# A second product of the one-hot tile with itself, ahead of the degree product, on TensorE during setup

## The reference, cut to what matters

```python
deg_out = segment_sum(w, s); deg_in = segment_sum(w, d)        # with self loops
wn = w * rsqrt(deg_out)[s] * rsqrt(deg_in)[d]
for _ in range(10):
    h = 0.9 * segment_sum(h[s] * wn[:, None], d) + 0.1 * feat_0
x = layernorm(x + h)
score = exp(clip(sum(K[src] * Q[dst] / sqrt(8) * E, -1), -5, 5))   # 8 heads of 8
x = layernorm(x + segment_sum(V[src] * score, dst))
```

## Time and profile before

| what | us |
|---|---|
| median of three runs | 9977.31 |
| the profiled execution's own time | 9976.81 |
| its span | 9975.0 |
| first degree product starts (line 2330) | 161.5 |
| last degree product starts (line 2330) | 1568.1 |
| flag is written (line 2092) | 1641.1 |

### The profile page before, as it was taken

The page is one execution under the profiler, slowest core; times in us unless marked ns, Lnnn a source line. Parts: engine busy times, 40 slices in busy tenths (PEclk is TensorE's granted clock), DMA queues, the critical chain, the costliest instruction groups (busy, mean ns, idle before and its releaser), DMA issues.

```text
span 9975.0 us, 144406 instructions
## 1 busy us (share of the span) xinstructions
PE 8829.3 (89%) x50368; PEld 4786.6 (48%) x50368; DVE 4943.6 (50%) x14438; ACT 5539.0 (56%) x7215; POOL 7255.4 (73%) x7701
## 2 busy tenths in 40 slices
PE   3999997999999999999999999999999766666666
PEld 2777774333333333333333333333333465655665
DVE  7666663443444434444344443444434455566666
ACT  1333334787777777777777777777777411111111
POOL 5677776777777777777777777777777377777776
PEclk5555556999999999999999999999999777777676
DMA  9972225999999999899999999999999565555554
GB/s 359 394 279 64 74 71 174 347 344 310 347 310 347 339 317 347 309 346 334 323 347 309 347 326 331 348 308 348 318 336 342 167 162 143 143 145 143 143 143 119
DMA packets 1378005, 2669.54 MB, mean 268 GB/s; under 512 B 683776, under 2 KB 713379, under 8 KB 1377270
## 3 DMA queue, kind: packets, MB, share of 16 engines
q1 hardware_dynamic: 958006, 2245.72, 63.3%
q0 software_dynamic: 248000, 261.74, 10.7%
q10 hardware_dynamic: 171264, 152.74, 5.3%
HBM read 2426.96 MB, written 232.42 MB: 267 GB/s over the span
## 4 chain that ended last, share of the span: by engine, by line
PE 42%; POOL 39%; issue 14%; DMA 3%; DVE 2%; ACT 1%; SPq 0%; POOLq 0%; DVEq 0%; ACTq 0%
PE banks L2369 25%; POOL arena L1646 23%; POOL arena L1660 15%; PE banks L2330 10%; PE banks L2420 3%; PE banks L2332 3%; DMA arena<-node_rows,src_idx 1%; PE banks L2413 1%; DMA x_sb<-in_edge_weight_dram 1%; PE banks L2447 1%; DMA u_sb<-key_rows 1%; DMA arena<-dense 0%; POOL dense L1622 0%; DVE arena L1934 0%; POOL arena L1642 0%
## 5 line engine op out<-in xcount | busy, mean ns | idle before, releaser
L1646 POOL DMA_INDIRECT arena<-node_rows,src_idx x4800 | 4582.3, 955 | 1583.8 <-issue 1452.0
L1716 ACT ACTIVATE arena<-arena 128x1024 f32<-128x1024 f32 x4900 | 4762.2, 1044 | 1380.2 <-DMA arena<-dense 1224.3
L2369 PE MATMUL banks<-arena 128*64 128x512 f32 x12240 | 2715.0, 595 | 19.8 <-ACT arena L1716 19.5
L2369 PE MATMUL banks<-arena,u_sb 128*64 128x512 f32 x11760 | 2613.1, 596 | 82.3 <-ACT arena L1716 82.0
L1660 POOL DMA_INDIRECT arena<-kv_rows,src_idx x1568 | 1503.1, 959 | 597.2 <-issue 477.7
L2103 DVE TENSOR_SCALAR arena<-banks,rel,w_tab 128x128 f32<-128x128 f32 x4800 | 1603.5, 403 | 123.2 <-DVE arena L2120 99.6
L2369 PEld LDWEIGHTS banks<-arena 128*64 128x64 f32 x12240 | 877.0, 138 | 1544.4 <-issue 1467.8
L2369 PEld LDWEIGHTS banks<-arena,u_sb 128*64 128x64 f32 x11760 | 844.4, 138 | 1552.3 <-issue 1467.6
L2330 PE MATMUL banks<-arena 128*128 128x98 f32 x3136 | 1174.7, 478 | 93.0 <-ACT arena L1695 92.9
L1622 POOL DMA_INDIRECT dense<-arena x1012 | 980.4, 969 | 370.8 <-issue 314.6
L1765 ACT ACTIVATE banks<-arena 128x64 f32<-128x64 f32 x196 | 44.6, 228 | 1694.6 <-DVEq L2248 1694.6
(11 more groups left out here) (241 smaller groups left out, 6399.4 us busy)
## 6 DMA issues: line engine op xcount, KB each, us to landing
arena<-dense SPq DMA_DIRECT2D x3550, 512.0 KB
dense<-blank SPq DMA_DIRECT2D x5, 26112.0 KB, 189.5
arena<-in_dst_dram SPq DMA_DIRECT2D x195, 512.0 KB
arena<-node_rows,src_idx POOLq DMA_INDIRECT x4800
arena<-in_edge_attr_dram SPq DMA_DIRECT2D x195, 256.0 KB, 3.2
u_sb<-key_rows ACTq DMA_DIRECT2D x26, 1792.0 KB
dense<-blank SPq DMA_DIRECT2D x1, 44800.0 KB, 195.0
arena<-key_rows ACTq DMA_DIRECT2D x23, 1792.0 KB
```

The source lines that it names most:

```text
L1646: gp.indirect_dma_start(out=rows_in[:, n % ROWS, s, :], out_offset=None, in_=node_rows[k % 2], in_offset=bass.IndirectOffsetOnAxis(ap=src_ ...
L1716: nc.scalar.activation(planes[:, q % PLANES, half, :], ring[:, n % SLOTS, :], ACT.Relu, scale=-1.0 if half else 1.0).then_inc(planes_act, 1)
L2369: done = mm(banks[h * D:(h + 1) * D, sum_slot(k, g), :], u, rows[:, h * 512:(h + 1) * 512], start=first, stop=last, tile_position=(0, h * ...
```

## The change

One product is added per tile in `setup_pe`, ahead of the wide degree product: `hot_lo` of the tile as weights (128 columns) and as the moving operand (128 columns), written to columns 0 to 127 of PSUM bank 0 with `start` and `stop` set. Nothing reads that result. No wait and no semaphore update is added or moved.

```diff
@@ -2325,6 +2325,7 @@
             pe.wait_ge(hots_scaled, n + 1)
             for t in range(HB):
                 col = n * HB + t
+                mm(banks[:, 0, 0:P], hot_lo[:, n % 2, t, :], hot_lo[:, n % 2, t, :], start=True, stop=True, skip_group_check=True)
                 s0 = BASE[col // 2] // QUART
                 end = n == HOT_BATCHES - 1
                 mm(banks[:, 4, 0:NB], hot_lo[:, n % 2, t, :], hot_hw[:, n % 2, t, 0:NB], start=False, stop=end and t == HB - 1, skip_group_check=True)
```

## The result

The changed kernel takes 10621.48 us (median of 4 runs, 10619.44 to 10627.08) against 9977.3 us, a ratio of 1.0645 with a 95% interval of 1.0631 to 1.0659. It is 644 us slower; the forecast was 648 us more, 10625 us. The profiled execution has a span of 10617.7 us, 642.7 more than before.

What follows compares the result with a forecast made beforehand. The prediction took TensorE to bound the setup loop at 1.2 GHz: 669 us for the added pairs less 21 us of filled idle time, 648 us more, gave 10625 us. The range was 10565 to 10685 us.

Steps and rivals of the forecast that it cites:

- TensorE is the bound of the setup and nothing hides the added work: Setup's degree-product loop: TensorE busy 250.00 of 250 us, so added products lengthen the setup, by 648 us net.
- the 32 that were given as the most: End of setup: GpSimd's scatters set the limit, so a faster TensorE could bring back at most 32 us.
- The price of the pair, two record paces of 0.213 us: Each tile of the degree-product loop grows by 0.427 us, from 0.88 to 1.31; 669 us over 1568 products.
- The second rival: Degree-product loop: the added pair costs more, 0.68 to 0.86 us, giving 11017 to 11300 us; chance 3%.
- The idle time that fills: Degree-product loop: the added work fills 21 of the 26.5 us that TensorE idles, which is taken off the cost.
- The clock stays at 1.2 GHz: Degree-product loop: TensorE's granted clock stays at 0.50 all through, despite the added products.
- The first rival: Degree-product loop: the added stream raises TensorE to 2.4 GHz, GpSimd sets the end, 9945 us; chance 6%.
- The third rival: Degree-product loop: shared weight loads leave 125 us of cost, 10100 us, chance 1%; costing nothing, 9977 us, another 1%.
- What follows the flag: Behind the setup's end, the propagation and the attention stay as long as before.

Runs made afterwards that it cites:

- grouped order: Against the kernel before, nothing added: a batch's eight wide degree products come first, then its eight narrow ones; 9958.1 us, ratio 0.9975.

## Why the prediction was right

**TensorE is the bound of the setup and nothing hides the added work: right.** The tile grew from 0.88 to 1.31 us, every added us in the loop beyond the idle time that it filled reached the flag, and half the products cost half. The grouped order is the other side of it: when TensorE's batch shrinks to 4.18 us, its share of the chain falls to 16% and 28.6 us come back at the flag, close to the 32 that were given as the most.

**The price of the pair, two record paces of 0.213 us: right, and for the reason given.** 1568 x 0.427 = 669 us. With 64 columns the time is the same, as the pace of the weight loads has it. A fixed time for every record is not it, as in the grouped order sixteen records with 32 weights columns, placed on the four quarters in turn, take 0.52 us. With 256 the stream is longer than the load and the price is the stream's, 0.853 us. The same runs show that the loads lie beside the streams: with load and stream one behind the other the tile would have taken 1.73 us, not 1.31. That is against the rule on row groups that the prediction cites from the Trainium skill's TensorE: Matmul & The Clock Gate, in its part on packing small matmuls; the same part also lets a load run ahead when it goes to a background weight buffer, which the prediction left out, and no run here tells which path the loads took. The second rival falls. The split within the tile was not told in advance: the wide pair behind the added one takes 0.52 us in place of 0.68, and the added pair 0.59.

**The idle time that fills: mis-sized by 5 us.** All of the 26.5 us went, not 21: 669 - 26.5 = 642.5, and the flag moved by 642.5. That the two agree so closely is partly chance, as the first product also starts 0.8 us later. This term made the forecast span, 10623 us, 5 us too high. The median came nearer, 3.5 us below the forecast, because it lies 2 us above the profiled execution.

**The clock stays at 1.2 GHz: right.** This was the term on which all else hung, and the argument was the right kind: not that TensorE is busy, which it is in both states, but what it ran in stretches of the attention before the clock rose and where it did not. It was not a near thing either: with twice the columns the clock still stays at 0.50. The first rival named the price of the other case correctly: at 2.4 GHz the old tile takes 0.55 us, the changed one 0.78, less than 0.88, and the time is that of GpSimd, 9954 us (9945 was given). It only did not happen by itself. The Trainium skill's rule that sustained activity releases the clock (TensorE: Matmul & The Clock Gate, its part on the clock gate) agrees with the kernel of 512 columns and with the grouped order that has the added product. It does not agree with the old order at 98, 128 and 256 columns, where TensorE counts as busy 250.00 of 250 us at 0.50.

**The third rival** (shared loads, or hidden) falls with the 3136 loads more in the profile's page and the 643 us.

**What follows the flag** did not change, as forecast.

The grouped order gained 25 us against 32 expected, and 28.6 at the flag. The difference between the two lies behind the flag, in a part that no edit touches: it takes 8332.1 to 8345.8 us in the profiled executions of all kernels, 8341.3 in this one and 8333.9 before. Of the rest, GpSimd still waits 3.1 of the 5.3 us for VectorE, and a scatter has a median of 0.972 us in place of 0.969, which is 3 us over 1012 of them.

What stays open: what in the alternation makes the old tile long. Narrow products load 32 weights columns, sit on a quarter of the array and write PSUM bank 5. The change of bank alone is not it, since the added and the wide product of the grouped order change between banks 0 and 4 and still run at 0.11 us a record at 2.4 GHz; the placement and the small loads were not separated. Also open is how long the tile of the change would keep the high clock, since no run leaves it more than seven batches (43 us) behind a wide one.

## What to carry to other kernels

In a loop of small float32 products on TensorE, count weight loads, and changes between wide and placed narrow products, before columns: sorting eight wide and eight narrow products into two groups took a batch from 7.04 to 4.18 us, with no work added. Work added to raise TensorE's clock pays only if the clock then does rise; read in the profile what the engine ran before a rise, and compare the new loop with that, since one that falls short pays for its padding in full (here 643 us). And ask first what a faster TensorE would be worth: here GpSimd stood 32 us behind it, so that padding could have gained no more than that.

## What the runs showed that I had not expected

The granted clock of one and the same instruction stream depends on what ran before it. Tiles of the change run at 1.00 for all seven batches, 43 us, behind a batch with 512 columns, and at 0.50 for the whole loop without one, or behind a wait of 7.79 us until the next wide batch. The old tiles, with nothing added, do not keep the high clock: behind the same wide batch they are back at 0.50 within some 5 us. So in these runs the added product of 128 columns kept the high clock over those 43 us, and never raised it.
